# A GNN megakernel on one core: order of PE's work in the sort, ACT's work moved to DVE in layer 0, and another layout of one store

## What is computed

```python
k_src = K[src] + rel_k[edge_type] + time_emb @ Wt + bt
euclid = jnp.sum(q_dst * k_src, axis=-1) / np.float32(np.sqrt(DH))
decay_raw = jnp.tanh(jax.nn.relu(dec_in @ Wd1 + bd1) @ Wd2 + bd2)
decay = jnp.exp(decay_scale[None, :] * decay_raw)
logits = alpha * (euclid * decay) + (1.0 - alpha) * hyp     # hyp = -beta * |m[src]-m[dst]| * decay
ex = jnp.exp(logits - seg_max[dst])
agg = jax.ops.segment_sum(v_src * (ex / denom[dst])[..., None], dst, num_segments=n)
```

## Time and profile before

| | us |
|---|---|
| median of 3 executions | 4250.34 (4250.27 to 4251.71) |
| the profiled execution, own time | 4250.27 |
| its span in the profile | 4248.5 |
| layer-0 loop, about | 199 to 1439 |
| join and node work of layer 0 | 1439 to 1654 |
| sort | 1654 to 2150 |
| layers 1 to 3 | 2150 to 4248 |

### The profile page before, as it was taken

One profiled execution on the slowest core, in us unless ns is written; L12 is line 12 of the kernel. 1 busy time (PEld: TensorE's weight loads), 2 busy tenths in 40 slices (PEclk: granted clock), 3 DMA queues, 4 the chain that ended last, 5 costly groups with the idle time before them and its releaser, 6 DMA issues.

```text
span 4248.5 us, 86373 instructions
## 1 busy us (share of the span) xinstructions
PE 3232.4 (76%) x31231; PEld 2711.3 (64%) x31231; DVE 3263.1 (77%) x6283; ACT 2208.4 (52%) x6574; POOL 2088.6 (49%) x2453
## 2 busy tenths in 40 slices
PE   1388888788888532677737788766999999689995
PEld 1155555555555321577636778744999999679995
DVE  5499988678888544999948878767666666779997
ACT  2377777677777322899925666621222222234443
POOL 0366777666666410599812200000555555368883
PEclk7699999999999766778868899978999999889998
DMA  4789899888888401000012211133444444223331
GB/s 91 230 231 257 258 264 262 203 249 257 258 258 256 114 14 41 6 14 13 11 34 90 69 45 44 41 122 105 122 125 124 122 131 124 77 74 129 129 128 63
DMA packets 397012, 550.62 MB, mean 130 GB/s; under 512 B 80169, under 2 KB 311275, under 8 KB 396443
## 3 DMA queue, kind: packets, MB, share of 16 engines
q1 hardware_dynamic: 342427, 380.67, 29.9%
q0 software_dynamic: 54144, 164.25, 13.8%
HBM read 433.68 MB, written 111.07 MB: 128 GB/s over the span
## 4 chain that ended last, share of the span: by engine, by line
PE 50%; DVE 26%; ACT 12%; issue 5%; DMA 3%; SPq 3%; POOL 1%; DVEq 0%; ACTq 0%; POOLq 0%
PE psum L2477 6%; PE psum L3759 5%; PE psum L2505 4%; PE psum L2497 4%; PE psum L3775 4%; PE psum L3710 4%; PE psum L3708 4%; ACT arena_a L1399 3%; PE psum L3675 2%; PE psum L3734 2%; DVE arena_a L3255 2%; ACT arena_c L1385 2%; PE psum L3347 2%; PE psum L3757 2%; PE psum L2487 2%
## 5 line engine op out<-in xcount | busy, mean ns | idle before, releaser
L1216 POOL DMA_INDIRECT arena_a<-src_table,src_tix x808 | 822.1, 1017 | 541.6 <-issue 385.2
L3479 POOL TENSOR_SCALAR node_hot<-arena_c 128x128 fp32r<-128x128 f32 x575 | 369.8, 654 | 900.1 <-DVE arena_c L3367 568.0
L3497 DVE SCALAR_TENSOR_TENSOR msg_parts<-psum,msg_parts 128x512 fp32r<-128x512 f32 (+2 forms) x644 | 425.3, 660 | 260.7 <-ACT msg_parts L3646 228.5
L3646 ACT ACTIVATE msg_parts<-psum 128x512 fp32r<-128x512 f32 (+2 forms) x325 | 186.4, 574 | 520.4 <-PE psum L3710 520.4
L3197 POOL TENSOR_SCALAR node_hot_dst<-arena_c 128x128 fp32r<-128x128 f32 x587 | 384.3, 671 | 122.1 <-DVE arena_c L3601 67.9
L3708 PE MATMUL psum<-arena_c,arena_a 128*128 128x128 bf16 x3675 | 406.4, 220 | 0.0
L3710 PE MATMUL psum<-arena_c,arena_a 128*128 128x128 bf16 x3675 | 406.4, 220 | 0.0
L1399 ACT ACTIVATE arena_a<-arena_a 128x128 f32<-128x128 f32 x808 | 238.7, 298 | 206.5 <-DVE arena_a L1906 204.4
L3706 PE MATMUL psum<-src_tix,arena_a 128*128 128x128 bf16 x1225 | 272.4, 222 | 70.9 <-DVE arena_a L3383 37.2
L3661 ACT ACTIVATE msg_parts<-psum 128x512 fp32r<-128x512 f32 (+1 forms) x319 | 185.4, 581 | 260.5 <-PE psum L3759 260.5
L3759 PE MATMUL psum<-arena_c,arena_a 128*128 128x128 bf16 x3675 | 308.9, 219 | 0.0
(11 more groups left out here) (606 smaller groups left out, 9968.2 us busy)
## 6 DMA issues: line engine op xcount, KB each, us to landing
y_rows<-arena_c SPq DMA_DIRECT2D x101, 576.0 KB
arena_a<-bucket_rows SPq DMA_DIRECT2D x150, 384.0 KB
arena_c<-near_keys SPq DMA_DIRECT2D x101, 256.0 KB
arena_b<-near_keys SPq DMA_DIRECT2D x101, 252.0 KB
arena_a<-bucket_rows SPq DMA_DIRECT2D x50, 448.0 KB
arena_a<-bucket_lists SPq DMA_DIRECT2D x25, 896.0 KB
pair_counts<-arena_c SPq DMA_DIRECT2D x25, 800.0 KB
arena_a<-bucket_lists SPq DMA_DIRECT2D x25, 704.0 KB
```

The source lines that it names most:

```text
L1216: e.indirect_dma_start(out_, None, table, bass.IndirectOffsetOnAxis(ap=idx, axis=0)).then_inc(sem, 16)
L3479: return e.tensor_scalar(node_hot[at % RING_M][:, i, :], iota_row, src_lo[:, b, 2 * k + j:2 * k + j + 1], None, ALU.is_equal)
L3497: e.scalar_tensor_tensor(out=to[:, 1, 0:nt, :], in0=bank[at % 4][:, 0:nt * P].rearrange("p (t f) -> p t f", f=P), scalar=0.0, in1=to[:, 0, ...
```

## The change

It does six things.
1. PE's order in the sort becomes prefix(n), sums(n-1), transposes(n-2), and ACT copies the turned rows of n-3, not n-4. The loops of both are one turn shorter.
2. The inverse 1 / (1 + x) in the decay net is made by DVE, with an addition and a reciprocal right after `dve_l0_messages`, in place of ACT's 1451 and 1462.
3. The keep-busy matmuls run for the last two blocks too.
4. Layer 0's store into `y_rows` gives each partition 8 consecutive rows, so a partition's 8 x 576 bytes are contiguous in DRAM. What was in row (tile, partition) comes to stand in row (partition x 8 + tile) of its block.
5. The join of layer 0 follows: the last rows are fetched with 16 DMAs, two for each tile number in a block, and POOL gathers by `y0_ix`, which DVE computes with five integer instructions from `end_ix`.
6. The semaphore count that PE's join waits for is raised accordingly.

```diff
@@ layer 0, the store and the join @@
+        def lane_rows(table, k):
+            return table[k * TPB * P:(k + 1) * TPB * P, :].rearrange("(p t) w -> p t w", t=TPB)
...
-            e.dma_start(edge_rows(y_rows[L], k), ybuf[s][:, :, 0:W_Y[L]]).then_inc(g.d_y[s], 16)
+            to = lane_rows(y_rows[L], k) if L == 0 else edge_rows(y_rows[L], k)
+            e.dma_start(to, ybuf[s][:, :, 0:W_Y[L]]).then_inc(g.d_y[s], 16)
...
+            if L == 0:
+                q_ = P // TPB
+                lasts = y_rows[L].rearrange("(k e) w -> k e w", e=TPB * P)[:, (P - 1) * TPB:, :]
+                for t in range(TPB):
+                    e.dma_start(LR[t:P:TPB, 0:TC - 1, :], lasts[0:(TC - 1) * q_, t, :].rearrange("(c q) w -> q c w", q=q_)).then_inc(g.d_ends, 16)
+                    e.dma_start(LR[t:REST:TPB, TC - 1, :], lasts[(TC - 1) * q_:NBLK, t, :]).then_inc(g.d_ends, 16)
...
+            y_ix = y0_ix if L == 0 else end_ix
             for b in range(NB):
-                pool_gather(e, YE[:, b, :], y_rows[L], end_ix[:, b:b + 1], g.d_nodeg)
+                pool_gather(e, YE[:, b, :], y_rows[L], y_ix[:, b:b + 1], g.d_nodeg)
@@ ACT, layer 0 @@
                 if b1:
-                    e.wait_ge(g.decay_exp, i1 + 1)
-                    e.activation(tlog[s1][:, 3, :], tlog[s1][:, 3, :], ACT.Ln, bias=1.0).then_inc(g.decay_inverse, 1)
                     act_w_squares(e, i1, 0)
...
-                if b1:
-                    e.wait_ge(g.decay_inverse, 2 * i1 + 1)
-                    e.activation(tlog[s1][:, 3, :], tlog[s1][:, 3, :], ACT.Exp, scale=-1.0).then_inc(g.decay_inverse, 1)
...
-                    e.wait_ge(g.decay_inverse, 2 * i1 + 2)
+                    e.wait_ge(g.decay_inverse, i1 + 1)
@@ DVE, layer 0 @@
+            own.step(e.tensor_scalar(tile_ix[:, :], end_ix[:, :], P - 1, 3, ALU.bitwise_and, ALU.logical_shift_left))
+            own.step(e.tensor_scalar(y0_ix[:, :], end_ix[:, :], -TPB * P, None, ALU.bitwise_and))
+            own.step(e.tensor_tensor(y0_ix[:, :], y0_ix[:, :], tile_ix[:, :], ALU.bitwise_or))
+            own.step(e.tensor_scalar(tile_ix[:, :], end_ix[:, :], 7, TPB - 1, ALU.arith_shift_right, ALU.bitwise_and))
+            own.step(e.tensor_tensor(y0_ix[:, :], y0_ix[:, :], tile_ix[:, :], ALU.bitwise_or))
...
                 if b3:
                     dve_l0_messages(e, i3)
+                if b1:
+                    e.wait_ge(g.decay_exp, i1 + 1)
+                    own.step(e.tensor_scalar(tlog[s1][:, 3, :], tlog[s1][:, 3, :], 1.0, None, ALU.add))
+                    e.reciprocal(tlog[s1][:, 3, :], tlog[s1][:, 3, :]).then_inc(g.decay_inverse, 1)
@@ PE, layer 0 and join @@
-                if b1 and i1 < NBLK - 2:
+                if b1:
                     pe_keep_busy(e, i1)
...
-            e.wait_ge(g.d_ends, 32 * (u + 1))
+            e.wait_ge(g.d_ends, 32 * (TPB + u))
@@ ACT, sort @@
-            for n in range(NB + 4):
+            for n in range(NB + 3):
...
-                if n >= 4:
-                    b = n - 4
+                if n >= 3:
+                    b = n - 3
@@ PE, sort @@
-            for n in range(-1, NB + 3):
-                if n + 1 < NB:
-                    b = n + 1
+            for n in range(NB + 2):
+                if n < NB:
...
-                if n >= 3:
-                    b = n - 3
...
                 if 0 <= n - 1 < NB:
...
+                if n >= 2:
+                    b = n - 2
...
```

More of the change, by code:

```diff
@@ L548, in program @@
         end_ix = sb("end_ix", [P, NB], I32)
+        y0_ix = sb("y0_ix", [P, NB], I32)
         tile_ix = sb("tile_ix", [P, NB], I32)
@@ L1048, in sp_join @@
             e.wait_ge(g.dve_through, phase)
-            lasts = y_rows[L].rearrange("(t e) w -> t e w", e=P)[:, P - 1, :]
-            e.dma_start(LR[:, 0:TC - 1, :], lasts[0:(TC - 1) * P, :].rearrange("(c p) w -> p c w", p=P)).then_inc(g.d_ends, 16)
-            e.dma_start(LR[0:REST, TC - 1, :], lasts[(TC - 1) * P:TT, :]).then_inc(g.d_ends, 16)
+            if L == 0:
[4 more added lines that the diff above has]
+                    e.dma_start(LR[t:REST:TPB, TC - 1, :], lasts[(TC - 1) * q_:NBLK, t, :]).then_inc(g.d_ends, 16)
+            else:
+                lasts = y_rows[L].rearrange("(t e) w -> t e w", e=P)[:, P - 1, :]
+                e.dma_start(LR[:, 0:TC - 1, :], lasts[0:(TC - 1) * P, :].rearrange("(c p) w -> p c w", p=P)).then_inc(g.d_ends, 16)
+                e.dma_start(LR[0:REST, TC - 1, :], lasts[(TC - 1) * P:TT, :]).then_inc(g.d_ends, 16)
             e.wait_ge(g.join_back, 6 * (j + 1) if L != 3 else 14)
@@ L3044, in pe_sort @@
             pause(e)
-            for n in range(-1, NB + 3):
-                if n + 1 < NB:
-                    b = n + 1
[L3048 to L3051, removed]
+            for n in range(NB + 2):
+                if n < NB:
+                    s = n % 2
+                    e.wait_ge(sig.tot_dve, n + 1)
+                    if n >= 2:
+                        e.wait_ge(sig.pre_used, n - 1)
                     e.matmul(bank[s][:, 0:NB], lower[:, :], tot[s], start=True, stop=True)
                     e.matmul(bank[6 + s][0:1, 0:NB], ones[:, 0:1], tot[s], start=True, stop=True).then_inc(sig.pre_pe, 1)
-                if n >= 3:
-                    b = n - 3
[L3056 to L3064, removed]
-                    t_.then_inc(sig.turned_pe, 1)
                 if 0 <= n - 1 < NB:
@@ L3076, in pe_sort @@
                     put.then_inc(sig.packed_pe, 1)
+                if n >= 2:
+                    b = n - 2
+                    s = b % 2
+                    turned = bank[4 + s][:, :].bitcast(BF16)
+                    e.wait_ge(sig.fields, b + 1)
+                    if b >= 2:
+                        e.wait_ge(sig.rows_act, b - 1)
+                    for i in range(5):
+                        m_ = 2 * KT if i < 4 else KT
+                        rows = field[s][:, 0:2, :] if i == 0 else attr_keep[b][:, 2 * i - 2:2 * i, :] if i < 4 else field[s][:, DL:DL + 1, :]
+                        t_ = e.transpose(turned[0:m_, i * P:(i + 1) * P], rows.rearrange("p f k -> p (f k)"), ident_h)
+                    t_.then_inc(sig.turned_pe, 1)
             e.wait_ge(sig.flag, 1)
```

## The result

The changed kernel takes 4300.43 us (median of 4, 4299.26 to 4302.95) against 4250.5 us beside it on the same chip: ratio 1.0116, 95% interval 1.0102 to 1.0132, 50 us slower. Its profiled execution has a span of 4298.9 us, 50.4 more than before. The forecast was 4306.6, 6 us too high.

The account below looks back on a forecast made before the run. It took PE then ACT to bound layer-0 blocks, DVE a near second, and DVE the sort. 37.7 + 22.7 - 10.2 - 2 + 1 + 1.6 + 5.5 = +56.3 on 4250.27 gives 4306.6 us, range 4280 to 4332.

Parts of the forecast that it names:

- The sort: Sort: the prefix stands behind transposes that wait for POOL, so DVE waits 1.7 us in each bucket; sum +37.7 us.
- Behind the last bucket: End of the sort: SP has two buckets' stores left behind the last sums, not three; -0.9 us.
- The inverse in blocks 1 to 25: Early layer-0 blocks: DVE has almost no gap for the added addition and reciprocal; 0.91 us each, +22.7 us.
- The inverse elsewhere: Other layer-0 blocks: ACT's 1462 leaves the chain and DVE's gap covers its added work; 0.14 us a block, -10.2 us.
- SP's hang: Halfway through the layer-0 loop, at SP's element-wise transfers: fewer packets ahead in its queue may help; -2 us (0 to -5).
- the index steps: Layer-0 loop, halfway: five more small integer steps on DVE; +1 us.
- Last turns: Last two layer-0 turns: keep-busy matmuls cost about +2.1 and +1.2, sums at the upper clock give -1.7; net +1.6 us.
- Join: Join of layer 0: SP issues 16 loads at some 0.43 us each, 6.9 us instead of 1.1; +5.5 us (0 to 9).
- (a): Rival, sort: it doesn't slow, as POOL finishes before 2937 and the prefix is there in time; 4269 us, chance 0.12.
- (b): Rival, sort: POOL gets less done beside DVE, or PE's lower clock stretches its work; 19.6 us a bucket, 4327 us, chance 0.08.
- (c): Rival, early layer-0 loop: added DVE work is free in blocks 2 to 26, being short or overlapping; 4284 us, chance 0.04.
- (d): Rival, layer-0 loop: transfers hold the 76 blocks that DVE doesn't bound, so it gets faster; 4214 us, chance 0.04.

Follow-up runs that it names:

- experiment 1: The changed kernel with the sort's order on PE and ACT put back as before; 4264.82 us, 1.0048 of the kernel before.
- experiment 2: The changed kernel with PE's sort order prefix(n+1), sums(n-1), transposes(n-2), so only the prefix goes ahead; 4263.18 us, 1.0045 of the kernel before.
- experiment 8: The changed kernel with POOL doing two of its 15 unpacking instructions after telling PE; second chip, 4898.47 us, 1.0054 of the kernel before.
- experiment 3: The changed kernel with the decay inverse made by ACT's ln and exp again; 4290.27 us, 1.01 of the kernel before.
- experiment 4: The changed kernel with layer 0's store, the join's loads, gather indices and semaphore count as before; 4286.9 us, 1.0089 of the kernel before.
- experiment 9: The changed kernel with the join's 16 loads written as 7, store layout kept; second chip, 4894.54 us, 1.0052 of the kernel before.

## Why the prediction was right, step by step

**The sort, +37.7 predicted, +29.2 measured.** The mechanism is shown, by experiments 1, 2 and 8. Its sizes:
- 20 buckets x 1.7 = 34: they came 18.30 us apart on average, against 16.90, so 20 x 1.40 = 28.0. The working gives 18.6, and 8 of the 20 are that long (18.53 to 18.59), as 1919.24 - 1900.71 = 18.53 here, with POOL ending 16.85 us after the start. I had 17.0: POOL's instructions went as worked out, nine of them before DVE's 2951, and the 0.15 is small amounts along the way. Another 8 take 18.0 to 18.1, and 4 lie between. POOL is no earlier in them (16.86), but PE is faster. The table by stretches, PE's transposes and prefix in a short and in a long bucket:

```profile
1899.50:1900.70 1.20, 1.06 (x9) 0.76 (x9) 0.00 (x0) 1.19 (x1) 0.05 (x1) 0.96 0.00 0
1917.50:1919.20 1.70, 1.59 (x9) 1.13 (x9) 0.00 (x0) 1.67 (x2) 0.06 (x1) 0.55 0.00 0
```

  The granted clock is 0.96 in the one and 0.55 in the other, so the same nine matmuls take 1.1 us or 1.6. From POOL's end to DVE's start it is 1.16 us in the buckets that have the upper of the clock's two levels throughout (granted 1.00, 2.4 GHz) and 1.72 in those at the lower (0.50, 1.2 GHz), on average 1.44. I had 1.6, the transposes' 0.95 from rows at a granted clock of 0.50 and the prefix's 0.55 from rows at 1.00. So the 0.3 us by which I was too high are half POOL's and half the clock's.
- First bucket that pays, +2.3 (3.4 predicted), and 0.3 in the one before it; last one, +2.6 (1.2).
- Behind the last bucket: 3.9 us less, where I had 0.9. With the last bucket's +2.6 that is -1.3, where I had +0.3. That PE and POOL have less left to do when DVE has been held up would explain it, but isn't shown; experiment 2, which holds nothing up, gives 1.8 there against experiment 1.

**The inverse in blocks 1 to 25, +22.7 predicted, +17.5 measured.** Mechanism shown by experiment 3. 0.70 us each, not 0.91. I had priced the pair at 1.18 us and the room for it at 0.27; the pair took 1.11 (its addition 0.21, not the 0.28 of the earlier trace rows), and the room was 0.42, as experiment 3's rows show: I had taken 0.60 us as the distance from a 1904 to the next instruction, which is 0.54 once they stand packed, and overlooked 0.08 ahead of 1904. The reciprocal was sized rightly by the row: 0.94. By the repeat count of the Trainium skill ("VectorE: DVE Perf Modes", "Walkthrough: the 8-slice pipeline in each mode") it was an estimate of 1.07, and the trace has 0.13 less.

**The inverse elsewhere, -10.2 predicted, -7.8 measured.** From block 26 to 50 it is 0.14 us a block, as worked out; from 54 on 0.10. In both the chain is no longer ACT's but goes through DVE, as the rows above show, so ACT's saving can't all be had. What differs is one instruction on that chain, the first of the two scans (1978): it takes 0.42 us on average in blocks 26 to 50 and 0.46 from 54 on, and every other step from block to block is equal within 0.01 us. Why it is longer there stays open.

**SP's hang, -2, and the index steps, +1:** +2.1 in that execution, within the spread of the others. Neither is shown.

**Last turns, +1.6:** +2.7 in this execution, +0.3 in three others and +3.0 in experiment 3. I had the last turn's matmuls at the upper level, 2.58 us, and three pairs of sums; they took 4.43 to 5.18, and five or seven pairs kept the level.

**Join, +5.5 predicted, +8.6 measured.** The count was right, the price was not: I had taken 0.43 us an issue; it was 0.675, above even the 0.64 of the one issue in the earlier trace rows. The issues take 10.8 us instead of 1.06, and 1.1 of the 9.7 comes back behind the last one. My upper bound, 9 us from that row, was the better value. Experiments 4 and 9 show it.

**The rivals.** (a), the sort doesn't slow, and (b), 19.6 us a bucket, are out by the buckets' 18.3. (c), free DVE work early, is out on the first chip; on the second, where a block is 18 us long, it cost nothing early, but there DVE has room (201 of 288 us busy), which isn't the reason that (c) gave. (d), the loop held by its transfers, is out on the first chip: 128 packets for 1024 a block changed its pace by nothing. By the Trainium skill ("DMA: Bandwidth & Descriptors", "Why small descriptors are slow"), which charges each packet a few cycles, some of the store's time should be had back; DMA engines are 0.02 to 0.05 less busy from 866 to 1400 us with the new layout (0.84 to 0.86, against 0.88 and 0.89), so the trace agrees, and no one waits for them.

The errors partly cancel: sort 8.5 and early blocks 5.2 too high, late blocks 2.4, SP and index steps 3.1, last turns 1.1, join 3.1 too low, and 1.8 us of small gains at the start of the loop and behind the join that I had not counted. Together 8.5 + 5.2 + 1.8 - 2.4 - 3.1 - 1.1 - 3.1 = 5.8 us, the distance from 56.3 to the table's 50.4 but for rounding. That the total came out near is in part luck; the signs and places of the four large terms are not. The bounds that the terms state add up to 4291 to 4317 with the sort at 1.7 us a bucket, not to 4290 to 4322; the result lies in either.

## What to carry to other kernels

In an in-order stream, look at what a result's maker now stands behind: the prefix takes half a microsecond and was ready a period early; put behind five transposes that wait for the slowest engine, it held the busiest one 1.4 us in each of 20 buckets. Work that moves to another engine costs what that engine has no gap for, stage by stage: the same two DVE instructions cost 0.70 us in 25 blocks and nothing in the others, and what the relieved engine gives back ends at the next chain, 0.10 to 0.14 us. Count DMA issues on the path before bytes: seven loads for sixteen gave 6 us back, and eight times fewer packets off the path gave none.

## What the runs showed of the hardware that I had not expected

- SP needs 0.37 to 0.83 us to issue one of the join's strided loads, one after the other, and 0.675 on average for the sixteen.
- One chip ran the same program 15% slower than another. Of the 618 us between the two profiles of the changed kernel some 600 are in the layer-0 loop, 9 ahead of it and 17 behind it up to the sort, and none in the sort or in layers 1 to 3. The change was worth 50 us on one and 41 or 46 on the other.
- PE's granted clock decided 0.56 us of an 18 us period of the sort: nine small matmuls on the path went at the lower level in 8 of 20 buckets, at the upper in 8, and at both in 4.
- On the second chip DVE and ACT, waiting for two products of PE, went on at the same moment some 5 us after PE's rows had ended, in 71 of 101 blocks.
